# A decoder layer on one core: cross-attention's first scores one step further ahead, rows normalised on ScalarE, two groups of loads placed elsewhere

## What is computed

```python
def _layernorm(x, axis=-1, eps=1e-05):
    m = jnp.mean(x, axis=axis, keepdims=True)
    v = jnp.var(x, axis=axis, keepdims=True)
    return (x - m) / jnp.sqrt(v + eps)
...
# cross-attention, per batch and head
rel = jnp.abs(jnp.arange(Nk)[None, :] - jnp.arange(Nq)[:, None] - (Nk - Nq))
bias = -slopes[:, None, None] * rel.astype(jnp.float32)
scores = jnp.einsum('bhqd,bhkd->bhqk', q, k) * scale + bias[None]
attn = jax.nn.softmax(scores, axis=-1)
out = jnp.einsum('bhqk,bhkd->bhqd', attn, v)
out = out.transpose(0, 2, 1, 3).reshape(B, Nq, E)
return out @ Wo + bo
...
x = x + _L0_attn_ref(_layernorm(x, axis=-1), ...)
x = x + _L0_xattn_ref(_layernorm(x, axis=-1), ctx_1024, ...)
x = x + _L0_ffn_ref(_layernorm(x, axis=-1), ...)
```

## Time and profile before

| | us |
|---|---|
| runs (median of 3) | 1738.88 (1736.13 to 1742.64) |
| the profiled execution | 1741.56 |
| its span, first to last instruction | 1739.8 |
| PE busy | 1661.7 (96%) |
| cross-attention's phase, about | 645 to 1112 |
| granted TensorE clock, mean | 0.985 |

### The profile page before, as it was taken

One profiled execution on the slowest core, in us unless ns is written; L12 is line 12 of the kernel. 1 busy time (PEld: TensorE's weight loads), 2 busy tenths in 40 slices (PEclk: granted clock), 3 DMA queues, 4 the chain that ended last, 5 costly groups with the idle time before them and its releaser, 6 DMA issues. The chain is left out here.

```text
span 1739.8 us, 34540 instructions
## 1 busy us (share of the span) xinstructions
PE 1661.7 (96%) x10934; PEld 1334.2 (77%) x10934; DVE 1079.5 (62%) x1897; ACT 748.1 (43%) x1348; POOL 754.5 (43%) x845
## 2 busy tenths in 40 slices
PE   9898999999999989899999989899999999999998
PEld 8786787888787767677777766678888888888876
DVE  6554566565656567788888888664564646436653
ACT  4224344444434427566565554523442424224441
POOL 3200423332333318788787665531451514215441
PEclk9999999999999999999999998899999999999999
DMA  7747665666666749998777874247564646356773
GB/s 243 254 152 218 179 191 173 193 195 208 180 187 198 189 119 184 206 208 169 151 158 149 172 153 152 87 125 232 182 185 149 196 128 220 102 163 186 244 245 91
DMA packets 207936, 309.50 MB, mean 178 GB/s; under 512 B 21592, under 2 KB 151336, under 8 KB 202944
## 3 DMA queue, kind: packets, MB, share of 16 engines
q1 hardware_dynamic: 188304, 227.16, 48.8%
q0 software_dynamic: 14768, 46.27, 10.8%
q10 hardware_dynamic: 4752, 34.61, 5.4%
HBM read 224.30 MB, written 83.66 MB: 177 GB/s over the span
## 5 line engine op out<-in xcount | busy, mean ns | idle before, releaser
L2216 DVE TENSOR_REDUCE part_max<-a_s_bank 112x1 f32<-112x500 f32 (+1 forms) x368 | 224.6, 668 | 62.9 <-PE a_s_bank L1936 49.2
L2111 ACT ACTIVATE a_prob<-a_st_bank 125x448 f32<-125x448 f32 x384 | 196.8, 546 | 112.2 <-PE a_st_bank L1959 94.7
L2922 DVE TENSOR_TENSOR e_u_sb<-e_u_bank,e_b_row 128x512 f32<-128x512 f32 x134 | 92.2, 688 | 230.4 <-PE e_u_bank L2679 217.8
L2677 PE MATMUL e_u_bank<-e_w_hi,e_xT_hi 128*128 128x512 f32 x536 | 214.3, 400 | 0.9 <-DVE e_w_lo L2915 0.4
L2678 PE MATMUL e_u_bank<-e_w_lo,e_xT_hi 128*128 128x512 f32 x536 | 209.9, 392 | 0.0
L2679 PE MATMUL e_u_bank<-e_w_hi,e_xT_lo 128*128 128x512 f32 x536 | 209.5, 391 | 0.0
L2738 ACT ACTIVATE e_g_hi<-e_g_bank 128x256 fp32r<-128x256 f32 x133 | 51.3, 385 | 342.5 <-PE e_g_bank L2686 340.5
L2839 POOL DMA_INDIRECT out<-l_rows,e_y_row x33 | 53.0, 1605 | 291.2 <-DVE l_rows L2965 148.5
L1786 POOL TENSOR_TENSOR a_part_sum<-a_prob 125x448 f32<-125x448 f32 x128 | 147.5, 1157 | 31.7 <-ACT a_prob L2111 31.4
L1028 POOL TENSOR_TENSOR m_prob_sum<-m_prob 112x224 f32<-112x224 f32 x128 | 93.9, 738 | 138.2 <-ACT m_prob L1270 130.0
L2815 POOL TENSOR_TENSOR e_w_lo<-e_w_raw,e_w_hi 128x1024 fp32r<-128x1024 f32 x28 | 102.6, 3674 | 48.9 <-ACT e_w_hi L2748 48.9
(11 more groups left out here) (438 smaller groups left out, 4309.9 us busy)
## 6 DMA issues: line engine op xcount, KB each, us to landing
e_w_raw<-L_ffn_Wl SPq DMA_DIRECT2D x96, 512.0 KB, 8.4
e_b_row<-L_ffn_bl ACTq DMA_DIRECT2D x33, 1024.0 KB
m_c_in<-ctx POOLq DMA_DIRECT2D x12, 1000.0 KB, 6.1
k<-m_kt_hi SPq DMA_DIRECT2D x48, 250.0 KB, 3.3
k<-m_kt_lo SPq DMA_DIRECT2D x48, 250.0 KB, 4.1
v<-m_cv SPq DMA_DIRECT2D x48, 224.0 KB
a_v_sb<-v SPq DMA_DIRECT2D x32, 336.0 KB
m_q_st<-q SPq DMA_DIRECT2D x93, 112.0 KB, 3.0
```

The costliest lines, as they stand in the source:

```text
L2111: act.activation(prob[s % 2][:, hh, 2 * u:2 * u + 2, :], st_bank[n % SB][0:CR, 0:2 * S].rearrange("p (e q) -> p e q", e=2), ACT.Exp).then_ ...
L2216: dve.tensor_reduce(out, scores, AX.X, ALU.max).then_inc(s_free, 1)
L2677: pe.matmul(out, xT_hi[:, slot, k, :], w_h, start=(k == 0), stop=False)
```

## The change

- `first_step(s)` is s + 3 from s = 1 on (s + 2 up to s = 0). Iteration s now computes `second_scores(s + 1)` with `first_scores(s + 3)`; the last iterations have one less of them, and iteration 0 gets a block of its own: all twelve units of `first_scores(3)`, behind its loop over the heads, with nothing between them but `turn_max(2)`. VectorE takes maxima in the same order, with `maxima(3)` and `row_maxima(3)` in a block.
- `turn_max(s + 2)` leaves `values(s)` and stands behind head 1's units from s = 1 on; ScalarE's `query_rows(s + 2)` moves from the iteration's end to behind head 1's exponentials. Four matmuls that ran before `turn_max(31)` are gone. `part_max` alternates between its two halves.
- For batches 0 to 6 ScalarE normalises the rows (`hidden_rows`, Identity with scale rstd and bias -mean x rstd, at hh 0 and 1); VectorE only makes the two columns (`inverse`), at the end of the iteration before. The residual of batch b waits for the rows of batch b - 1.
- The output weights and bias are issued in SP's iteration 1, behind `load_qk(5)` and `load_v(4)`.
- In the opening GpSimd waits for v's tiles before each of its last three loads: chunk 1's last before `m_wv`, chunk 2's first before `m_wq`, chunk 2's last before the context.

```diff
@@ -363,8 +363,12 @@
                     if hh == 1:
                         load_x(2)
                 load_x(3)
+                pool.wait_ge(o_free, prod_at["wv", 1, TT - 1] + 1)
                 load_w_behind("m_wv", "wo")
+                pool.wait_ge(o_free, prod_at["wv", 2, 0] + 1)
                 load_w_behind("m_wq", "m_wk")
+                pool.wait_ge(o_free, prod_at["wv", 2, TT - 1] + 1)
+                pool.sem_inc(turn, 1)
                 pool.dma_start(c_in[:, :, :], ctx[0]).then_inc(ctx_loaded, DMA)
                 pool.wait_ge(row_step, ROW_STEPS)
                 pool.sem_inc(turn, 1)
@@ -1505,13 +1509,20 @@
     for hh in range(4):
         note(s_at, "s", 0, hh, RP - 1)
     note(st_at, "max", 0)
+    def first_step(s):
+
+        step = s + 2 if s < 1 else s + 3
+        return step if step < STEPS else None
+
     for s in range(-1, STEPS):
         for hh in range(4):
             for n in range(RP):
                 if s + 1 < STEPS:
                     note(st_at, "s", s + 1, hh, n)
-                if s + 2 < STEPS and n in first_units(s + 2):
-                    note(s_at, "s", s + 2, hh, n)
+                if first_step(s) is not None and n in first_units(first_step(s)):
+                    note(s_at, "s", first_step(s), hh, n)
+            if s >= 1 and s + 2 < STEPS and hh == 1:
+                note(st_at, "max", s + 2)
             if s == 2 and hh == 3:
                 note(st_at, "wr")
             if s >= 5 and s % 4 == 1 and hh % 2 == 0:
...
@@ -1523,8 +1534,12 @@
                 note(s_at, "route", (s - 7) // 4)
             if s in GOES and hh == RANKED[s]:
                 note(s_at, "rank", s)
-        if s + 2 < STEPS:
+        if s < 1:
             note(st_at, "max", s + 2)
+        if s == 0:
+            for hh in range(4):
+                for n in range(RP):
+                    note(s_at, "s", 3, hh, n)
...
+        shift = c.sb("a_shift", [QR, 2])
...
@@ -1723,14 +1740,15 @@
                 sp.dma_start(wr_raw[:, :], w_route).then_inc(small_loaded, DMA)
                 load_qk(SLOTS)
                 load_v(SLOTS - 1)
-                sp.dma_start(w_raw[:, :, :], w_out.rearrange("(k p) n -> p k n", p=P)).then_inc(w_loaded, DMA)
-                sp.dma_start(out_bias[:, :], b_out.partition_broadcast(P)).then_inc(bias_loaded, DMA)
                 for s in range(STEPS):
                     if s + SLOTS < STEPS and s:
                         load_qk(s + SLOTS)
                         load_v(s + SLOTS - 1)
                     elif s + SLOTS == STEPS:
                         load_v(STEPS - 1)
+                    if s == 1:
+                        sp.dma_start(w_raw[:, :, :], w_out.rearrange("(k p) n -> p k n", p=P)).then_inc(w_loaded, DMA)
+                        sp.dma_start(out_bias[:, :], b_out.partition_broadcast(P)).then_inc(bias_loaded, DMA)
...
@@ -1969,8 +1987,6 @@
                     bank = st_next("max", s)
                     if s < 2:
                         keep_clock_early(bank, 6 - 3 * s, s)
-                    elif s == 31:
-                        keep_clock(bank, 4)
...
-                    if s + 2 < STEPS:
-                        turn_max(s + 2)
...
@@ -2065,8 +2079,10 @@
                         for n in range(RP):
                             if s + 1 < STEPS:
                                 second_scores(s + 1, hh, n)
-                            if s + 2 < STEPS and n in first_units(s + 2):
-                                first_scores(s + 2, hh, n)
+                            if first_step(s) is not None and n in first_units(first_step(s)):
+                                first_scores(first_step(s), hh, n)
+                        if s >= 1 and s + 2 < STEPS and hh == 1:
+                            turn_max(s + 2)
...
@@ -2077,10 +2093,18 @@
                             route(batch_at(s, 3))
                         if s in GOES and hh == RANKED[s]:
                             ranks(s)
+                    if s == 0:
+                        for hh in range(2):
+                            for n in range(RP):
+                                first_scores(3, hh, n)
+                    if s < 1:
+                        turn_max(s + 2)
+                    if s == 0:
+                        for hh in range(2, 4):
+                            for n in range(RP):
+                                first_scores(3, hh, n)
                     if s >= 0:
                         values(s)
-                    else:
-                        turn_max(1)
...
+
+                def hidden_rows(b, t):
+                    act.wait_ge(shift_ready, b + 1)
+                    act.activation(xh[b % 2][:, t, :], x_new[:, t, :], ACT.Identity, bias=shift[:, t:t + 1], scale=rstd[:, t:t + 1]).then_inc(h_ready, 1)
...
                         for n in range(RP):
                             if s + 1 < STEPS:
                                 exp(s + 1, hh, n)
+                        if s >= 1 and s + 2 < STEPS and hh == 1:
+                            query_rows(s + 2)
...
+                        if hh < 2 and batch_at(s, 2) is not None:
+                            hidden_rows(batch_at(s, 2), hh)
...
                     if batch_at(s, 1) is not None:
                         root(batch_at(s, 1))
-                    if s + 2 < STEPS:
+                    if s < 1:
                         query_rows(s + 2)
...
@@ -2209,9 +2241,9 @@
                         at = s_at["s", s, hh, n]
                         bank = s_bank[at % SB][0:QR, :]
                         if n < 2:
-                            out, scores = part_max[:, 1 if s == 1 else 0, hh, n, 0:1], bank[:, 0:LIN]
+                            out, scores = part_max[:, s % 2, hh, n, 0:1], bank[:, 0:LIN]
                         else:
-                            out, scores = part_max[:, 1 if s == 1 else 0, hh, :, 1], bank[:, 0:2 * FAR].rearrange("p (t k) -> p t k", t=2)
+                            out, scores = part_max[:, s % 2, hh, :, 1], bank[:, 0:2 * FAR].rearrange("p (t k) -> p t k", t=2)
...
@@ -2240,6 +2272,7 @@
                             dve.wait_ge(last_xb_ready, 1)
                         if b:
                             dve.wait_ge(x2_stored, b * DMA)
+                            dve.wait_ge(h_ready, 2 * b)
...
+
+                def inverse(b):
+                    dve.wait_ge(std_done, b + 1)
+                    dve.reciprocal(rstd[:, :], std[:, :]).then_inc(rstd_done, 1)
+                    dve.wait_ge(rstd_done, b + 1)
+                    dve.scalar_tensor_tensor(shift[:, :], mv[:, :, 0], -1.0, rstd[:, :], ALU.mult, ALU.mult).then_inc(shift_ready, 1)
...
@@ -2370,8 +2409,8 @@
                                 dve.wait_ge(small_loaded, 3 * DMA)
                             dve.wait_ge(whi_ready, hh + 1)
                             dve.tensor_tensor(w_lo[:, hh, :], w_raw[:, hh, :], as_f32(w_hi[:, hh, :]), ALU.subtract).then_inc(w_ready, 1)
-                        if s + 2 < STEPS:
-                            maxima(s + 2, hh)
+                        if first_step(s) is not None:
+                            maxima(first_step(s), hh)
...
-                        if hh % 2 == 0 and batch_at(s, 2) is not None:
-                            hidden(batch_at(s, 2), (hh // 2,))
...
@@ -2421,10 +2458,16 @@
                             slots(20, 0)
                         if s == 28 and hh >= 2:
                             slots(28, hh - 2)
-                    if s + 2 < STEPS:
-                        row_maxima(s + 2)
+                    if first_step(s) is not None:
+                        row_maxima(first_step(s))
+                    if s == 0:
+                        for hh in range(4):
+                            maxima(3, hh)
+                        row_maxima(3)
                     if 1 <= s < STEPS - 1:
                         normalise(s - 1)
+                    if batch_at(s, 1) is not None:
+                        inverse(batch_at(s, 1))
```

3 lines of the change are left out of this document (2 added, 1 removed).

## The result

The median of seven runs is 1723.51 us (1721.45 to 1724.19) beside 1736.13 (1729.55 to 1742.64) for the kernel before: a ratio of 0.9923, 95% interval 0.9899 to 0.9948, clear of 1; 12.6 us less by the medians. The forecast was 9.3 us less. On another chip the changed kernel had 1723.53 and a ratio of 0.9947 (0.9922 to 0.9973).

The account below looks back on a forecast made before the run. TensorE is busy 96% of the span, so time is saved mainly where it waits or runs at half clock; -6.0 + 11 - 3.2 - 4.7 - 1.2 + 2 - 5.2 - 2 = -9.3, median 1729.6, range 1716 to 1746.

Parts of the forecast that it names:

- The size and the place of the early loss: Iterations 0 to 4: stall moves to step 6's keys in iteration 3, ending at 711.7; +11 us, bounds +6 to +14.
- The gain from the weights is not seen: Iterations 0 to 4: moving the weights saves 6.7 us before step 5's keys, but step 6's keys stall instead.
- the block in iteration 0: Iteration 0: twelve units of first scores, TensorE waiting for VectorE's maxima (7.17 us), cost nothing while a load is later anyway.
- Opening: Opening: spacing loads between tiles of v removes TensorE's 4.45 us wait and 1.5 of low clock; -6.0, bounds -4 to -7.
- Copy in the middle: Twenty non-normalising iterations: ScalarE's copy among exponentials costs 0.3 each, +6.0, less 4.0 of waits removed; +2 us net.
- rival D: ScalarE becomes the bound: exponentials behind the copy late by 0.91 in 26 iterations, +17.7, giving 1747.3; chance 0.10.
- Normalising on ScalarE: Six normalising iterations: moving rows from VectorE to ScalarE gives 13.3 instead of 14.17 each; -5.2, bounds 0 to -10.
- most of the way to 12.0: Six normalising iterations: the favourable bound, -10, where 6 x 2.17 = 13.0 would reach 12.0 us each.
- The floor of 12.0: Steady iterations: one that only routes takes 12.0 us; what stands above it is wait and lower clock.
- Iterations 27 and 28: Iteration 27: half of the 4.21 us stall behind VectorE's small addition goes; -2, bounds +1 to -6.8.
- rival B: Iteration 27: its stall goes altogether as the two operations no longer meet; -6.8 instead of -2, 1724.8; chance 0.12.
- The last iterations: End: last first scores move from iteration 29 to 28, -3.2 (bounds -1 to -4); removed half-clock matmuls before last transposes, -1.2.

Follow-up runs that it names:

- the second profile: The changed kernel timed and profiled again with no edit: 1723.53 us.

## Why the prediction was right, and where it was off

- **The size and the place of the early loss** held. The forecast had the stall move from step 5's keys to step 6's, with iterations -1 to 4 longer by 11; measured are +11.4, and the stall ends 66.1 us behind the start of cross-attention (55.0 before; forecast 711.7 - 646.2 = 65.5). "The gain from the weights is not seen" is shown by the two kernels with the weights elsewhere. That the block in iteration 0 costs nothing since a load is late anyway also fits: iteration 0 grew by 10.7 us, in time that the keys were awaited in any case, and the stall behind it is as long as the one before. Where the load is no longer late, the block does cost: with v later iteration 0 takes 18.8 us, and 10.5 in the kernel without lookahead that has v later too (10.5 to 13.6 in all without the block), some 5 to 8 us, and no wait for a load stands behind it to cover it. The whole stretches (83.8 us with v later; 79.0 without lookahead, 83.1 without it and with v later) do not price the block, since each of the latter two has a stall of its own, of 5.44 and of 8.32 us. The forecast mixed KB of 1024 bytes with GB/s of 10^9, which makes its transfers 2% too short, 0.2 us in each.
- **Opening**: forecast -6.0; -4.3 in this pair of profiles, 6.4 apart over fourteen. The mechanism was right; the size can't be told to 2 us from a single pair of profiles.
- **Copy in the middle**: by all signs mis-signed. I took 0.3 us for each plain iteration. In the changed kernel a plain iteration takes 10.4 us instead of 10.6 with it, though it has the further lookahead as well, and no run moved the copy alone. ACT's timeline shows that it can't cost much there (iteration 8): the six exponentials before the copy and the six behind it have no idle time between them and the copy, and ScalarE then waits for TensorE for 3.43 us (the last row).

```profile
773.18 3.13 ACT L2135 ACTIVATE a_prob<-a_st_bank 125x448 f32<-125x448 f32 x6 [3.43 <-PE a_st_bank L1977]
776.34 0.91 ACT L2127 ACTIVATE third<-a_st_bank 8x896 fp32r<-8x896 f32 x1
777.27 2.86 ACT L2135 ACTIVATE a_prob<-a_st_bank 125x448 f32<-125x448 f32 x6
783.57 0.55 ACT L2135 ACTIVATE a_prob<-a_st_bank 125x448 f32<-125x448 f32 x1 [3.43 <-PE a_st_bank L1977]
```

Where ScalarE has the rows as well, the six iterations are longer with the copy there: 75.4 us, 72.7 and 71.3 without. These two kernels differ in the transposes' place too, and one in the lookahead, so that the copy is the likely cause and not a shown one. If it is, rival D was the right mechanism in the wrong iterations, 0.5 to 0.7 in six, not 0.91 in 26.
- **Normalising on ScalarE**: mis-sized. Forecast -5.2, measured -9.6 in the changed kernel and -13.4 alone, or -5.8 and -9.6 against the lowest profile of the old code. By the larger figures the bound that I gave ("most of the way to 12.0", -10 and 13.0) was nearer than the middle. The price was read from the operation (1.28 beside 0.77 us) instead of from what stands behind it on VectorE: the maxima, on which TensorE's first scores wait: 12.0 us before, 2.3 with this edit alone. The floor of 12.0 for an iteration was that of a routing one; these went down to 11.9 (71.6 / 6). The rule of the Trainium skill that was weighed (its page "ScalarE: Activation LUTs", Rules for kernel authors: add and multiply on VectorE) would have made it a loss; here VectorE was the engine that TensorE waited for.
- **Iterations 27 and 28**: -8.5 instead of -2, which was priced for 27 alone. That one went from 18.8 to 13.9 us (12.7 in the second profile), and 28 from 17.2 to 13.6 (16.8). The run with the opening alone has the same code there as before and shows 28.5 for both instead of 36.0, so the stall depends on how operations happen to meet, and the change is not needed to part them. It is there in two of fourteen profiles, with 36.0 us and with the small addition at 3.98 and 3.23 us; in the other twelve the addition takes 0.18 to 0.20 us and the two iterations 27.5 to 31.0. The -4.9 and -6.1 of iteration 27 are nearer to rival B's -6.8 than to -2, but not by the change. This is probably most of the distance between the profiles' 17.9 and the medians' 12.6; the other executions left no trace.
- **The last iterations**: -2.4 instead of -4.4, of which -3.2 was the missing first scores. Iteration 29, where both terms lie, fell by 3.4, from 18.7 to 15.3; iterations 30 and 31 rose from 19.4 to 20.4, with the clock at 0.82 before and 0.83 after.
- **The sum**: by the profiles it was off by 9 us (-18.6 measured, -9.3 said), mostly in the steady iterations (7) and in 27 and 28 (6.5); by the medians by 3.3, since the profiled execution of before lies 5.4 us above its median of seven and not 2.7. That the median came so near is in part luck: the forecast priced a profile, and the profile fell by twice as much.

**Which edit did what**, by medians on the same chip: the rows on ScalarE -12.2 alone (ratio 0.9923; taken out of the change they leave 1.0012); the opening -7.0 alone (ratio 0.997, so about -5); weights 0; lookahead with early transposes +6.4. The lowest median is that of the changed kernel with v two steps later, 1715.42 us: 8.1 below the changed kernel and 17.4 below the kernel before beside it. Its four runs do not tell it from the kernel without lookahead (1717.10, ratios 0.990 and 0.9916 with overlapping intervals).

**Left open**: what makes VectorE's operation take anything from 536 to 1930 ns. GpSimd's additions ran beside the long addition of the earlier trace rows, and no run took them away. Whether lookahead pays once the loads of v are later and the block of iteration 0 is spread over two iterations was not tried.

## What to carry to other kernels

Where the transfers of a stretch are bound by their rate, as here, the order in which they stand mostly chooses who waits: count the bytes ahead of the last one that is needed, and see what needn't be among them. An operation moved off the engine that others wait for is worth what stands behind it there, not the difference of its two durations. Before a stall is priced into a sum, see in a second profile of the same code whether it is there at all.

## What the runs showed of the hardware that I had not expected

The 16 DMA engines, at a busy share of 1.08 to 1.12, moved 182 to 191 GB/s in the stretches of cross-attention shown above, and 409 GB/s at a share of 1.04 with the large loads of the opening: the share does not tell the rate. The transfers of cross-attention are in packets of 3000, 896, 512 and 2048 bytes, but their size is not the whole cause. Packets of one size, 2048 bytes, took a mean of 85 ns at 70 to 80 us in the kernel before and 167 ns at 650 to 700 us, by the packet records of its trace. What makes them slower there is open; the size adds to it, as 512 bytes took 60 ns there and 3000 bytes 266, a third more for each byte.

And one shape of one VectorE operation took 536 ns at best and 1930 at worst in the same kernel, where ScalarE's version of it stayed between 802 and 831.
